# A bilinear tower on one core: VectorE multiplies two neighbouring PSUM banks in one instruction

## The reference

```python
e = jnp.stack([tbl_0[ids[:, 0]], ..., tbl_39[ids[:, 39]]], axis=1)
out = jnp.einsum('bie,fie,bif->bi', p, param, q)   # p = e[:, rowidx], q = e[:, colidx]
h = jnp.concatenate([z, dense_ctx], axis=1)
h = jnp.maximum(h @ W_top1 + b_top1, 0.0)
h = jnp.maximum(h @ W_top2 + b_top2, 0.0)
y = h @ W_top3
```

## Time and profile before

| what | value |
|---|---|
| median of 3 timed runs | 1217.54 us (1216.63 to 1221.66) |
| span of the profiled execution | 1255.3 us |
| TensorE matmul busy (PE) | 1224.6 us, 98% |
| VectorE busy (DVE) | 1053.7 us, 84% |
| ScalarE busy (ACT) | 972.3 us, 77% |
| GpSimd busy (POOL) | 573.2 us, 46% |
| granted TensorE clock, mean | 0.989 |

### The profile page before, as it was taken

How to read it: one execution, slowest core, us unless ns; L and a number is a source line. 1 busy time by engine, 2 the same in 40 slices (tenths; PEclk the granted TensorE clock), 3 DMA queues, 4 the chain that set the end, 5 groups by cost and what they waited for, 6 DMA issues and landing times.

```text
span 1255.3 us, 22898 instructions
## 1 busy us (share of the span) xinstructions
PE 1224.6 (98%) x5808; PEld 476.8 (38%) x5808; DVE 1053.7 (84%) x1720; ACT 972.3 (77%) x7177; POOL 573.2 (46%) x607
## 2 busy tenths in 40 slices
PE   6989999999999999999999999999999999999999
PEld 3323433333333333333333433334333334333333
DVE  6858899988888797889998888788999878899980
ACT  0019999975868887898968988799968988899951
POOL 5655554455455555555245555555245555400000
PEclk9988899999999999999999999999999999999999
DMA  7033344433544333333454433333353434122100
GB/s 207 18 113 104 79 119 117 110 104 92 140 100 120 102 104 87 88 81 97 106 134 106 113 84 94 87 80 96 95 155 90 114 97 111 49 63 83 44 1 1
DMA packets 132098, 118.87 MB, mean 95 GB/s; under 512 B 91351, under 2 KB 110039, under 8 KB 131965
## 3 DMA queue, kind: packets, MB, share of 16 engines
q1 hardware_dynamic: 111188, 94.94, 27.3%
q0 software_dynamic: 19200, 19.70, 7.6%
q10 hardware_dynamic: 1576, 2.76, 0.8%
HBM read 80.09 MB, written 0.01 MB: 64 GB/s over the span
## 4 chain that ended last, share of the span: by engine, by line
PE 88%; ACT 7%; issue 2%; DVE 2%; DMA 1%; SPq 0%; ACTq 0%; DVEq 0%
PE ring L793 40%; PE z_ps L816 18%; PE ring L798 17%; PE ring L822 8%; ACT wide_prod L606 6%; PE ring L756 2%; PE ring L826 2%; DVE prod L671 1%; DMA z_t<-tbl 1%; DVE wide_prod L685 0%; ACT e_t L567 0%; PE ring L774 0%; PE ring L829 0%; ACT h L620 0%; PE ring L767 0%
## 5 line engine op out<-in xcount | busy, mean ns | idle before, releaser
L606 ACT ACTIVATE wide_prod<-wide_prod 128x64 f32<-128x64 f32 x3520 | 841.8, 242 | 55.1 <-DVE wide_prod L685 34.8
L537 POOL DMA_INDIRECT rows<-tbl,idx_now x600 | 572.4, 954 | 514.9 <-DMA rows<-tbl,idx_now 310.0
L671 DVE TENSOR_TENSOR prod<-ring,e_t 128x512 f32<-128x512 f32 x1008 | 630.6, 683 | 114.3 <-PE ring L793 97.0
L606 ACT ACTIVATION_READ_ACCUMULATOR wide_prod<-wide_prod 128x1 f32 x3520 | 662.6, 188 | 17.8 <-issue 17.1
L793 PE MATMUL ring<-e_t,w 64*128 64x512 f32 x2176 | 584.3, 613 | 13.6 <-issue 4.8
L685 DVE TENSOR_TENSOR wide_prod<-ring,rows 128x512 f32<-128x512 f32 x512 | 327.8, 682 | 32.1 <-PE ring L798 12.8
L793 PEld LDWEIGHTS ring<-e_t,w 64*128 64x128 f32 x2176 | 229.0, 187 | 326.0 <-issue 210.0
L798 PE MATMUL ring<-w,e_t 64*128 64x512 f32 x1024 | 305.8, 616 | 4.2 <-DVE wide_prod L685 1.8
L816 PE MATMUL z_ps<-prod,strip 128*32 128x512 f32 x2096 | 253.9, 598 | 0.0
L798 PEld LDWEIGHTS ring<-w,e_t 64*128 64x128 f32 x1024 | 116.2, 189 | 150.5 <-issue 85.9
L816 PEld LDWEIGHTS z_ps<-prod,strip 128*32 128x32 f32 x2096 | 55.0, 109 | 179.7 <-issue 117.0
(11 more groups left out here) (24 smaller groups left out, 76.4 us busy)
## 6 DMA issues: line engine op xcount, KB each, us to landing
w<-weights SPq DMA_DIRECT2D x64, 768.0 KB
planes<-words SPq DMA_DIRECT2D x284, 64.0 KB
rows<-tbl,idx_now POOLq DMA_INDIRECT x600
z_t<-tbl SPq DMA_DIRECT2D x10, 224.0 KB
w<-weights SPq DMA_DIRECT2D x4, 512.0 KB
w<-hot_ids ACTq DMA_DIRECT2D x7, 256.0 KB
w<-w1z SPq DMA_DIRECT2D x7, 256.0 KB
words<-rows SPq DMA_TRANSPOSE x71
```

Source lines behind the costliest of these rows:

```text
L537: nc.gpsimd.indirect_dma_start(out=fields([tile], slice(slot, slot + 1), t)[:, 0, f, :], out_offset=None, in_=tables[m * 2 + f], in_offset ...
L606: last = nc.scalar.activation(products, products, ACT.Copy, accum_out=z_b[:, h, t, col:col + 1])
L671: nc.vector.tensor_tensor(dst[:, j, :], ring[:, bank, :], e_t[:, k, :], ALU.mult).then_inc(t_free, 1)
```

## The change

Where an item's two banks are neighbours in the ring (the first is bank b, the second b+1), VectorE waits for both blocks and multiplies them in one instruction of 1024 elements a partition; `e_t` (or the gathered rows) is read twice through a dimension of step 0. The instruction releases both banks with one increment of `t_free` at its end. Items that have bank 6 and bank 0, and diagonal units, keep two instructions and two increments. Of the 800 items 654 are joined (433 units and 221 wides), 106 others wrap round the ring and 40 are diagonal. Since the counts of `t_free` are no longer two an item, a list `FREED` holds the count behind each item, and all who waited for `through(n)` of `t_free` wait for `FREED[n]`.

```diff
+def joined(n):
+    _, kind, i = ITEMS[n]
+    low, high = BANKS["item", n]
+    return high == low + 1 and (kind == "wide" or UNITS[i][0] != UNITS[i][1])
+
+FREED = list(itertools.accumulate(1 if joined(n) else 2 for n in range(ALL_ITEMS)))
...
+        def runs_of_rows(c, t):
+            fixed = rows[:, fixed_slot(c):fixed_slot(c) + FIXED, :]
+            if by_dma(c * TILES):
+                runs = fixed.rearrange("p k (f t e) -> p (k f) t e", f=2, t=BT)[:, :, t, :]
+            else:
+                runs = fixed.rearrange("p k (t f e) -> p k t (f e)", f=2, t=BT)[:, :, t, :]
+            return runs.unsqueeze(1).broadcast_to([P, 2, *runs.shape[1:]])
...
                 dst, banks = prod[:, number % PROD_SLOTS, :, :], BANKS["item", n]
+                if joined(n):
+                    dve.wait_ge(t_ready, through(n))
+                    nc.vector.tensor_tensor(dst, ring[:, banks[0]:banks[0] + 2, :], e_t[:, k:k + 1, :].broadcast_to([P, 2, NB]),
+                                            ALU.mult).then_inc(t_free, 1)
+                    return
                 for j, bank in enumerate(banks):
...
+                banks = BANKS["item", n]
+                if joined(n):
+                    dve.wait_ge(t_ready, through(n))
+                    runs = runs_of_rows(c, t)
+                    length = runs.shape[-1]
+                    nc.vector.tensor_tensor(
+                        wide_prod[:, number % WIDE_SLOTS, :, :].rearrange("p j (q e) -> p j q e", e=length),
+                        ring[:, banks[0]:banks[0] + 2, :].rearrange("p j (q e) -> p j q e", e=length),
+                        runs, ALU.mult).then_inc(t_free, 1)
+                    return
...
-                        pe.wait_ge(t_free, 2 * n + BANKS[before].index(bank) + 1)
+                        pe.wait_ge(t_free, FREED[n] if joined(n) else FREED[n] - 1 + BANKS[before].index(bank))
...
-                pe.wait_ge(t_free, through(last_of_group(group)))
+                pe.wait_ge(t_free, FREED[last_of_group(group)])
```

More of the change, by code:

```diff
@@ L1 @@
+import itertools
 from contextlib import ExitStack
@@ L524, in _ @@
                 if m < FIXED and use > 1:
-                    pool.wait_ge(t_free, through(PLACE[c - 2, "wide", NW - 1]))
+                    pool.wait_ge(t_free, FREED[PLACE[c - 2, "wide", NW - 1]])
                 elif use > 1:
@@ L559, in prepare @@
                 if c > 0:
-                    act.wait_ge(t_free, through(last_reader(c - 1, m)))
+                    act.wait_ge(t_free, FREED[last_reader(c - 1, m)])
                 if by_dma(tile):
@@ L600, in reduce @@
                     act.wait_ge(turned, (c - 1) * HALVES + h + 1)
-                act.wait_ge(t_free, through(PLACE[c, "wide", v]))
+                act.wait_ge(t_free, FREED[PLACE[c, "wide", v]])
                 for jj in range(2):
@@ L682, in wide @@
                 fixed = [c * TILES + k for k in range(FIXED)]
-                for j, bank in enumerate(BANKS["item", n]):
+                banks = BANKS["item", n]
[8 more added lines that the diff above has]
+                    return
+                for j, bank in enumerate(banks):
                     dve.wait_ge(t_ready, 2 * n + j + 1)
@@ L694, in reduce @@
                     dve.wait_ge(turned, (c - 1) * HALVES + h + 1)
-                dve.wait_ge(t_free, through(n))
+                dve.wait_ge(t_free, FREED[n])
                 nc.vector.tensor_reduce(z_b[:, h, t, first:first + WIDE_PAIRS],
```

## The result

The changed kernel takes 1239.99 us (median of 4 runs, 1237.72 to 1241.83), the kernel before 1217.21 on the same chip. The ratio is 1.0197 with a 95% interval of 1.017 to 1.0223: 22.8 us slower. The forecast was 1248, 30 us slower. In the later runs one execution of the kernel before (4980.51 us) and one of a variant (4646.86 us) took about four times as long as the others; they are left out of every ratio and interval.

A forecast was written before the change was run, and what follows sets the result against it. The prediction took the bank loop between TensorE and VectorE as the bound. Terms 28 + 3.5 + 3 + 3 + 2 - 5 - 4 = 30 us on the median 1217.54 gave 1248 us, own range 1232 to 1262.

The forecast's parts named there:

- The bound: Loop between TensorE and VectorE through seven banks binds: sum group, first result, VectorE, freed bank, last item, sum group.
- VectorE's saving: VectorE's joined multiplications: 0.065 us less an item, 43 us of work over 654; time gained only where VectorE is never dry.
- the rival with a price of its own: Joined instruction costs a pair's 1.20 us or more because it crosses a bank; 1266 us, chance 13%.
- The second bank: VectorE's wait for an item's second block: free in most places, half a dozen late ones cost 3 us.
- The late release: First bank freed 0.53 us later, less 0.065 per joined item since VectorE was dry; holds the last item before a sum group.
- the quiet period: Sum group to sum group in the stretch from 1197.67 to 1204.94: 7.27 us before, 7.73 predicted, 0.46 later.
- The count: Lateness over 128 sum groups plus smaller terms: 28 + 3.5 + 3 + 3 + 2 - 5 - 4 = 30 us.
- 65 times 0.43: 65 sum groups with the item three back joined and slack under 0.1 lose 0.43 us on average, 28 us.
- The -4 us for lateness hidden behind those late results: Behind many middle sum groups the first result comes over 1.5 us late, so some lateness may hide there: -4 us.
- ScalarE and the gathers: ScalarE's reductions wait for the same last release, 0.07 us earlier; 77% busy, slower items leave it more room; no cost given.
- Faster: Rival: VectorE binds and its work pays; 1175 us with every joined item on the path, 1196 with half; chance 7%.
- No change: Rival: saving and lateness cancel, 1217 +- 6 us; chance 8%.

The follow-up runs named there:

- the experiment: Kernel before, but the first multiplication of the 654 items waits for both blocks, releases staying one a bank: 1221.82 us, ratio 1.0025.
- The two experiments with 0.60 and 0.53: Kernel before with both banks of the 654 items released after the second multiplication: 1253.43 us; the changed kernel with only 124 items joined: 1246.32 us.
- second profile: Kernel before, unchanged, profiled again: span 1221.2 us.
- first profile: Kernel before, unchanged, the profile on which the prediction rests: span 1255.3 us, 37.8 above its median.

## Why the prediction was right, step by step

**The bound.** Right. The loop through the ring was named as the bound, neither engine by itself; VectorE's 41 us of work less, and no gain from it, show it.

**VectorE's saving.** 0.065 us an item was predicted from the reduction; the joined rows take 1.217, and where VectorE is fed they start 1.131 apart, a pair 1.196 (medians): 0.065. Crossing a bank costs nothing that these rows show (the reduction of 1024 takes 1.209), so the rival with a price of its own is out. The figure of the Trainium skill (Perfetto Trace Analysis, Optimizing Scalar/DVE Operations), about 125 ns an operation on PSUM, isn't what is saved per operation here: back to back, half of it is. The 1238 that the prediction works out from it lies nearer to the measured 1240 than the forecast does, but by luck: the saving it supposes isn't there.

**The second bank.** 3 us predicted; the experiment has it at 3 by the ratio, with an interval from -2 to +8, and its profile at 2 from the 231st item on. Small in any case.

**The late release.** Right in place, and in size where the last item had no slack. 0.46 us a period was worked out, 7.73 for the quiet period; measured 0.47 and 7.74. The two experiments with 0.60 and 0.53, beside the change with 0.47, separate its parts.

**The count.** Here sizes were off. I took the difference after less before (second profile) of the time from each sum group to the next, for the groups in the classes of the prediction:

| class | groups | predicted us | measured us |
|---|---|---|---|
| item three back joined, slack under 0.1 | 64 | 28 | 18.6 |
| joined, slack 0.1 to 0.5 | 23 | 3.5 | 6.0 |
| joined, slack over 0.5 | 17 | 0 | 1.2 |
| item three back not joined | 23 | 0 | 0.6 |

(The period with the long gather wait, -7.2, is left out; with it the first class has the 65 groups of the prediction, which took the last two classes for 20 groups each. Steps and turns lie between sum groups, so their predicted 3 us, the late second banks and the held loads are in the measured column too.) Together 26.4. The unjoined ones stay at nothing, which is the theory's sharpest trace in the change itself.

The first class is too big because its slack was read from the long first profile, where late results had pushed many periods to the limit: in the second profile only 39 of the joined periods have a slack under 0.1, and 43 have 0.1 to 0.5. So the term "65 times 0.43" was mis-sized by its count, and the class with slack is more frequent than counted and dearer: the same rule, put to the second profile, gives 6.4 us for those 43 where 11.9 were measured, and 15.0 for the 39 where 12.5 were.

Why the rule is short for the class with slack can be seen in the matmuls of the last item. In 32 of the 43 periods that item has a slack of about 0.35, and 0.24 to 0.29 are lost. Such an item in before and in after (chain in order of time; the sum group follows at 1156.30 and at 1172.64):

```profile
1155.44 0.86 PE ring L798 x4
...
1171.54 1.10 PE ring L834 x4
```

Before, its four matmuls start at 0, 0.01, 0.43 and 0.44; in after at 0, 0.15, 0.43 and 0.68. The late bank holds the second block by 0.14, which is what the rule counts, and then the second pass of that block comes 0.53 behind its first instead of 0.43: a block that is held no longer runs side by side with its partner, and that is 0.1 us more, which the rule lacks.

The -4 us for lateness hidden behind those late results had its reason in them too and falls with them. So does the profiled span of 1285, which was carried over from the long profile: it was 1238.7.

**The term that was missing.** The prediction has one line on "ScalarE and the gathers", which gives a reason for ScalarE alone, and puts no cost or gain to either. The gathers hold TensorE in before, for 8.7 us in three places, and the change uses up most of that wait: the distance of the medians grows by 6.5 us when it is gone. In the first profile there is no such wait, since TensorE was already late there for other reasons. Without the wait the loss is 29 us, near the 30 of the sum: it came out by errors that cancel (the first class and the absorptions too big, the class with slack too small, the gathers missing), not because every term was good.

**The rivals.** Faster: out, with the saving fully there and none of it on the path. No change: out by its interval. The rule in the same section of the Trainium skill, that breaking up instructions may let work finish sooner where VectorE isn't saturated but causes bubbles on another engine, is borne out here: one longer instruction in 124 places is enough for the whole loss.

## What to carry to other kernels

An instruction that frees two buffers frees the first one late. Before merging, look for the consumer that takes that very buffer and ask what follows it: with a ring of 3.5 items and a stretch of work on the whole array behind it, half an item's delay came back in every period in which that consumer had no slack. Merge only where nobody waits for the first buffer (here a gain of 0.3% at best), and take the profile of before twice when its span lies well off the timed runs, since slack is read from it.

## What the hardware did that I hadn't expected

One VectorE multiplication over two neighbouring PSUM banks, with the other operand read twice through a step of 0, takes 1217 ns for 1024 elements, in both forms, where 512 take 682: no price for the bank's border. And two executions of one kernel differed by 34 us under the profiler (1255.3 and 1221.2) with the granted clock at 0.989 in both; the difference lay for a good part in first results behind sum groups, nearly all of them less than 1.8 us late, which I can't explain.
